# Attention scores of two heads as two 64-row tiles of TensorE, with queries that carry no zero rows

## The reference

```
q, k, v = split(einsum('bsd,od->bso', layernorm(x), w_project))
att = einsum('bhqd,bhkd->bhqk', q, k) / sqrt(16)
att = where(key > query, -1e9, att)
out = einsum('bhqk,bhkd->bhqd', softmax(att), v)
x   = x + einsum('bsd,od->bso', heads_joined(out), w_out)
```

## Time and profile before

| | |
|---|---|
| three runs, us | 1108.15, 1111.14, 1112.74 |
| median, us | 1111.14 |
| span of the profiled execution, us | 1107.3 |
| TensorE busy | 1029.0 us, 93% |
| VectorE busy | 714.0 us, 64% |
| ScalarE busy | 447.6 us, 40% |
| attention phase, us of the span | 379.6 to 845.0 |

### The profile page before, as it was taken

How to read it: one execution, slowest core, us unless ns; L and a number is a source line. 1 busy time by engine, 2 the same in 40 slices (tenths; PEclk the granted TensorE clock), 3 DMA queues, 4 the chain that set the end, 5 groups by cost and what they waited for, 6 DMA issues and landing times.

```text
span 1107.3 us, 16107 instructions
## 1 busy us (share of the span) xinstructions
PE 1029.0 (93%) x6208; PEld 473.7 (43%) x6208; DVE 714.0 (64%) x1128; ACT 447.6 (40%) x859; POOL 119.3 (11%) x147
## 2 busy tenths in 40 slices
PE   1779999999999599999999999999999999999998
PEld 1335545454555344333333333333324454544544
DVE  4786273654645588888887898887802836546362
ACT  1324020211214256555567666677786212112020
POOL 3665410000133000100000000000000100001000
PEclk9988999999999799999999999999999999999999
DMA  7000000000019600200020000000000000000000
GB/s 234 0 1 1 1 1 1 0 0 1 1 38 141 136 11 2 30 2 1 1 31 2 1 1 2 1 2 1 1 1 1 1 1 20 1 19 0 20 1 20
DMA packets 21964, 20.19 MB, mean 18 GB/s; under 512 B 4232, under 2 KB 21640, under 8 KB 21896
## 3 DMA queue, kind: packets, MB, share of 16 engines
q1 hardware_dynamic: 19784, 17.17, 7.5%
q10 hardware_dynamic: 2112, 2.10, 0.6%
HBM read 12.78 MB, written 6.29 MB: 17 GB/s over the span
## 4 chain that ended last, share of the span: by engine, by line
PE 82%; DVE 9%; issue 2%; POOL 2%; DMA 2%; ACT 1%; SPq 0%; DVEq 0%; ACTq 0%; POOLq 0%
PE ps L1037 12%; PE ps L940 10%; PE ps L1001 10%; PE ps L1023 10%; PE ps L908 10%; PE ps L909 10%; PE ps L910 10%; PE ps L941 5%; DVE m_part L820 4%; PE ps L1010 2%; DMA qk_split<-wreg 2%; PE ps L902 1%; PE ps L893 1%; PE ps L969 1%; DVE oT L626 1%
## 5 line engine op out<-in xcount | busy, mean ns | idle before, releaser
L563 ACT ACTIVATE wreg<-ps 128x512 f32<-128x512 f32 (+3 forms) x640 | 304.1, 536 | 152.9 <-PE ps L1023 78.0
L820 DVE TENSOR_REDUCE m_part<-ps 128x1 f32<-128x1024 f32 (+7 forms) x320 | 326.6, 1060 | 58.2 <-PE ps L1010 29.9
L519 ACT ACTIVATE wreg<-ps,gelu_in 128x512 f32<-128x512 f32 x128 | 88.0, 687 | 351.5 <-PE ps L910 351.5
L1023 PE MATMUL ps<-qreg,kreg 128*128 128x512 f16 (+3 forms) x640 | 181.0, 351 | 10.4 <-DMA qreg<-m_rows 8.7
L691 DVE SCALAR_TENSOR_TENSOR wreg<-ps,kappa,wreg 128x512 f32<-128x512 f32 x128 | 96.0, 750 | 145.6 <-PE ps L910 145.5
L1001 PE MATMUL ps<-kreg,qreg 128*128 128x512 f16 (+3 forms) x640 | 175.3, 351 | 7.7 <-DVE m_part L820 5.6
L940 PE MATMUL ps<-wd,qreg 128*128 128x512 f16 x512 | 166.8, 379 | 0.0
L1037 PE MATMUL ps<-wreg,v 128*17 128x512 f32 (+3 forms) x1280 | 149.8, 534 | 0.8 <-ACT oT L493 0.8
L941 PE MATMUL ps<-wd,qreg 128*128 128x256 f16 x512 | 139.6, 273 | 0.0
L1023 PEld LDWEIGHTS ps<-qreg,kreg 128*128 128x128 f16 x640 | 58.9, 97 | 131.1 <-ACT wreg L563 91.4
L908 PE MATMUL ps<-xT,wg 128*128 128x512 f16 x256 | 98.8, 386 | 3.1 <-DVE xT L671 2.4
(11 more groups left out here) (126 smaller groups left out, 931.4 us busy)
## 6 DMA issues: line engine op xcount, KB each, us to landing
qk_split<-wreg SPq DMA_DIRECT2D x4, 1024.0 KB, 9.1
kreg<-qk_split SPq DMA_DIRECT2D x24, 128.0 KB, 4.1
qreg<-qk_split SPq DMA_DIRECT2D x24, 128.0 KB, 7.8
xres<-in_L_attn_x ACTq DMA_DIRECT2D x4, 512.0 KB, 7.6
out_x<-xres SPq DMA_DIRECT2D x4, 512.0 KB, 2.9
kreg<-in_L_ffn_gate_W_packed SPq DMA_DIRECT2D x1, 1024.0 KB, 6.8
kreg<-in_L_ffn_up_W_packed SPq DMA_DIRECT2D x1, 1024.0 KB, 9.3
kreg<-in_L_ffn_down_W_packed SPq DMA_DIRECT2D x1, 1024.0 KB, 10.2
```

The costliest lines, as they stand in the source:

```text
L519: act.activation(gelu_ring[:, n % 3, :], bank(n % 2), ACT.Gelu_apprx_tanh, scale=gelu_in[:, 0:1]).then_inc(s_gelu, 1)
L563: act.activation(wreg[:, b % 8, 0:CT - q0], bank(score_bank[b], CT - q0), ACT.Exp, scale=EXP_SCALE).then_inc(s_p, 1)
L820: dve.tensor_reduce(m_part[:, r, part, col:col + 8 * (cnt - 1) + 1:8], src, AX.X, ALU.max)\
L1023: last = pe.matmul(dst, kreg[:, pair, P * j:P * j + P], qreg[:, c % 2, h % 2, pair, q0:CT], start=True, stop=not diag)
```

## The change

A matmul of scores no longer contracts all 128 partitions. It takes the 48 rows (50 with the maximum) of its own head, on partitions 0 to 63 or 64 to 127, and two such matmuls, one a head of the pair, stand next to each other in the program with their results in two banks. The mask is added in the same way, in two halves of 64 rows for each head: four matmuls of 64 columns a pair, in place of two of 128. Queries are stored once, in the first half of `inter`; the zeroing of line 465 and the transfers of line 322 go, and the first query load waits for the last products of feed-forward 1 instead. On GpSimd the small constants take ten `affine_select` in place of three. A unit of maxima is now always the two heads of a pair over at most 512 keys (`w` columns each), and the maxima of `c + 1` parts are joined by one reduction in "negate". In a step the two pairs of heads are the parts, with `weighted_values` between them. On the diagonal, both exponentials of a pair are released together, behind the masks.

```diff
-            units = []
-            for q in range(TPC):
...
+            return [(TPC * c + q, hp, CT * part, min(CT, P * (TPC * c + q + 1) - CT * part), part)
+                    for q in range(TPC) for part in range(c + 1) for hp in range(2)]
...
-                    sp.wait_ge(s_qzero, 1)
+                    sp.wait_ge(s_down_done, 1 + TPC * NCH)
...
-                if job == NCH + 1:
-                    pool.wait_ge(s_down_done, 1 + TPC * NCH)
-                    pool.memset(qflat.bitcast(i32), 0).then_inc(s_qzero, 1)
-                    pool.wait_ge(s_qzero, 1)
...
-                    if c >= 2:
-                        own(dve.tensor_tensor(m, m, m_part[:, r, 1, :], ALU.max))
+                    if c:
+                        m = m_all[:, r, :]
+                        own(dve.tensor_reduce(m, m_part[:, r, 0:c + 1, :].rearrange("p j k -> p k j"), AX.X, ALU.max))
...
+                    for a in range(2):
+                        rows = slice(64 * a, 64 * a + 3 * HD)
+                        last = pe.matmul(bank(at + a, w), qreg[rows, c % 2, pair, q0:q0 + P], kreg[rows, pair, k0:k0 + w],
+                                         start=True, stop=part < c)
+                    if part == c:
+                        last = masked([bank(at + a, P, diag) for a in range(2)], tri_a)
...
-                return pe.matmul(dst, tri[:, :], big_id[:, :], start=False, stop=True)
-
-            def scores(t, h):
+                for u in range(2):
+                    for a in range(2):
+                        rows = slice(64 * a, 64 * a + 64)
+                        last = pe.matmul(dst[a][:, 64 * u:64 * u + 64], tri[rows, u, :], big_id[rows, :],
+                                         start=False, stop=u == 1)
+                return last
+
+            def scores(t, hp):
...
+                for a in range(2):
+                    b = GH * t + 2 * hp + a
+                    if last_in_bank[b] is not None:
+                        pe.wait_ge(s_p, last_in_bank[b] + 1)
...
+                    rows = slice(64 * a, 64 * a + 3 * HD + 2)
+                    dst.append(bank(score_bank[b], CT - q0))
+                    last = pe.matmul(dst[a], kreg[rows, pair, P * j:P * j + P], qreg[rows, c % 2, pair, q0:CT],
+                                     start=True, stop=j < TPC * c)
+                    if j < TPC * c:
+                        last.then_inc(s_score, 1)
+                if j >= TPC * c:
+                    masked(dst, tri_b).then_inc(s_score, 2)
...
-                parts = [lambda: (scores(t, 0), scores(t, 1)), lambda: scores(t, 2), lambda: scores(t, 3)]
+                parts = [lambda: scores(t, 0), lambda: scores(t, 1)]
                 if t:
-                    parts.insert(2, lambda: weighted_values(t - 1))
+                    parts.insert(1, lambda: weighted_values(t - 1))
```

More of the change, by code:

```diff
@@ L151, in macaron_block @@
         s_qstack = [sem(f"query_stacks_in{k}") for k in range(NCH)]
-        s_qzero = sem("query_stacks_zeroed")
         s_slot, s_slot_read = sem("slot_written"), sem("slot_read")
@@ L191, in max_units @@
         def max_units(c, g):
-            units = []
-            for q in range(TPC):
[L197 to L211, removed]
+            return [(TPC * c + q, hp, CT * part, min(CT, P * (TPC * c + q + 1) - CT * part), part)
+                    for q in range(TPC) for part in range(c + 1) for hp in range(2)]
         def columns(unit):
-            return sum(k1 - k0 for _, _, k0, k1 in unit[2][0]) + 128
+            return 2 * unit[2][3] + 128
         def step_columns(t):
@@ L317, in load_queries @@
                         r = 64 * half + HD * row
-                        sp.dma_start(qreg[r:r + HD, c % 2, half, :, :],
+                        sp.dma_start(qreg[r:r + HD, c % 2, :, :],
                                      stack_source(c, 0, half, (0, 1, 0)[row])).then_inc(s_qstack[c], 16)
-                    if c >= 2:
[L321 to L324, removed]
             sp.wait_ge(s_ones, 1)
@@ L813, in maxima @@
                 else:
[L814 to L821, removed]
+                    i, hp, _, width, part = unit
+                    src = ps[:, 512 * at:512 * at + 1024].rearrange("p (a n) -> p a n", a=2)[:, :, 0:width]
+                    col = TPC * hp + i % TPC
+                    dve.tensor_reduce(m_part[:, r, part, col:col + 9:8], src, AX.X, ALU.max).then_inc(s_slot_read, 1)
                     read[0] = slot[0] + 1
@@ L990, in planned @@
                 else:
-                    if g == 0 and unit[2][1:3] == (0, 0) and unit[2][0] == 0:
+                    i, hp, k0, w, part = unit
+                    if g == 0 and unit[0:3] == (TPC * c, 0, 0):
                         pe.wait_ge(s_kstack[c], 16 * 6)
-                        pe.wait_ge(s_qstack[c], 16 * (6 if c < 2 else 8))
-                    for k, (h, i, k0, k1) in enumerate(unit[0]):
-                        pair = 2 * g + h // 2
-                        for m in range(k0, k1, 512):
-                            w = min(512, k1 - m)
-                            dst = bank(at + k + (m - k0) // 512, w)
-                            diag = P * i - m
-                            q0 = P * (i - TPC * c)
-                            last = pe.matmul(dst, qreg[:, c % 2, h % 2, pair, q0:q0 + P], kreg[:, pair, m:m + w],
-                                             start=True, stop=not 0 <= diag < w)
-                            if 0 <= diag < w:
-                                last = masked(dst[:, diag:diag + P], tri_a)
+                        pe.wait_ge(s_qstack[c], 16 * 6)
+                    pair = 2 * g + hp
+                    q0, diag = P * (i - TPC * c), P * i - k0
+                    for a in range(2):
[4 more added lines that the diff above has]
+                        last = masked([bank(at + a, P, diag) for a in range(2)], tri_a)
                 last.then_inc(s_slot, 1)
```

55 lines of the change are left out of this document (23 added, 32 removed).

## The result

The change made the kernel slower by 0.6%: 1115.6 us against 1110.4 us, medians of 11 runs each, ratio 1.0059 with a 95% interval of 1.0043 to 1.0075. The medians lie 5.2 us apart; 0.59% would be 6.5. I had forecast 1108 us and no change. The 11 runs go with the granted clock of TensorE over the span: the fastest, 1112.3 us, has 0.972, and the slowest, 1124.2 us, 0.957.

The account below looks back on a forecast made before the run. Bound by TensorE in regular groups, VectorE nearly as full in some stretches, ScalarE in the last group. Terms -3.4 - 3 - 4 + 7 + 0 = -3.4 us on 1111.1 gave about 1108 us, range 1102 to 1115 (8 in 10: 1086 to 1130).

Parts of the forecast that it names:

- Overlap of the pairs: Attention's score and unit matmuls on TensorE: two 64-row matmuls run together, a pair costing 0.216 us instead of 0.43.
- The rival that denied it: Attention's matmul pairs: no overlap, narrow matmuls cost by number; 1149 us, or 1125 with half of it; chance 0.22.
- The chain of waits: Full attention steps: weighted values wait for head 3's exponential, 2.78 us against 2.81 before, so the saved 0.87 becomes waiting.
- VectorE was not the bound: Rival in attention: a shorter chain lets TensorE's slack reach the maxima, VectorE bounds; 1070 us, likelier 1090; chance 0.34.
- my signs for it: Full steps: last head of weighted values waits about 0.6 us, TensorE's attention share 75% or less, step 2.75 to 2.9 us.
- The last group: Attention's last group, where ScalarE is full: ScalarE idles 0.52 us a full step; +7 us, bounds 0 and +11.
- full steps -3.4: 84 full steps outside the last group, in chunks 1 to 3: -0.04 us each, -3.4 in all, bounds -12 and +21.
- diagonal ones 11 x -0.2: Diagonal steps, four a group: -0.2 us in each of 15 groups, -3 in all, bounds -9 and +8.
- Stretches that VectorE fills: Three groups with `o`, `split`, `project`: -1 us each; denser steps of chunks 0 to 2: -1; sum -4, bounds -15 and 0.
- the clock as a rival: Attention on TensorE: granted clock falls for a third of the phase as its busy share drops; +65, 1175 us; chance 0.04.
- Before attention: Stretch before attention: zeroing of 6.93 us goes, but the transfer queue sets the end; 0 us, bounds -1.5 and 0.

Follow-up runs that it names:

- e2: The kernel before, with full-height matmuls and zero padding, given only the new order of scores and weighted values: 1133.5 us, ratio to before 1.0226.
- e3: The changed kernel, with weighted values behind both pairs of scores in the last group alone: 1108.1 us, ratio to before 0.9996.
- e10: The changed kernel, with every score matmul of chunk 0 issued twice to give TensorE more work: 1116.2 us, ratio to before 1.0063.
- e8: The changed kernel, with the old zeroing back on GpSimd and the old wait of the first query load: 1118.9 us, ratio to before 1.0083.
- e1: The changed kernel with the old order in a step, all on 64-row tiles: 1084.2 us, ratio to before 0.9769.

## Why the prediction was wrong, point by point

- *Overlap of the pairs*: right, 0.22 us a pair of 512 columns. The rival that denied it is out.
- *The chain of waits*: right, and it is the reason why the saving vanished. Forecast 2.78 us a full step, 2.82 with masks; measured 2.75, and 43.3 us for the regular group of chunk 3 (before 43.8). VectorE was not the bound; it idles 0.39 us a step. e2 shows the chain alone, 2.97 us in full height, where I expected 3.0. Two of my signs for it were wrong all the same. Of the 0.6 us of waiting that I put on the last head of the weighted values, they hold 0.16, and 0.40 stands at score 1's bank. And TensorE's busy share of attention is 86% (406.2 of 473.3 us), not 75% or less: in the last group it reads 36.3 of 37.0 us busy while the weighted values take twice their own time, so this share hides the waiting.
- *The last group*: right, +6.5 for +7; ScalarE's gap 0.46 us for 0.52; e3 took it away.
- *The middle*: near the forecast where the clock stayed. Of my terms about -9 fell on it (full steps -3.4, diagonal ones 11 x -0.2, VectorE's stretches about -3.5), and it gave -5.0 in the profiled run, but -4.5 in e3, -6.5 in e10 and -8.1 in e8, which have the same program there. The difference lies in groups with short spells of the lower clock: the first group of chunk 2 took 39.5 us at 0.96 and 38.3 at 1.00 (e8, e10), its third 34.8 at 0.95 and 33.6 at 1.00, and the first of chunk 1 29.1 at 0.93 and 28.0 at 1.00. With the shortest time of each group the middle would be at -8.6. So what is missing here belongs to the next point.
- *Chunk 0, and TensorE's clock*: this is the step that failed. In "Stretches that VectorE fills" I gave chunk 0 a part of -1, and the diagonal term another -0.8; it took +6.4 in the profiled run and +4.0 and +5.1 in e3 and e8, which are the same program up to there. What I had left out is that TensorE, finishing sooner in a stretch bound by VectorE, ran at a lower granted clock there (0.60 in group 2, where the kernel before has 1.00), and weighted values that take 1.84 us in place of 0.98 then starve VectorE (1.69 us idle). How much of group 2's loss is the clock and how much the order stays open. I had the clock as a rival, but with gaps of half a microsecond I didn't expect it; I priced it for a third of the phase, +65 us, and gave it 4%. It came in short stretches and cost a few microseconds.
- *Before attention*: normalisation came 1.5 us sooner and the queue set the start, as worked out, but my bounds of -1.5 and 0 missed. The profiled run has +2.1, of which 1.1 is feed-forward 1 ending later, which varies by more than that between the traces. Counted from the normalisation ahead of the zeroing, attention starts after 57.5 us (56.5 before), and after 56.6 to 58.0 in all ten tiled kernels without the zeroing. In that stretch the third chunk's store of 1 MB, which the key loads wait for, took 12.6 us in place of 10.5 (before, then changed):

```profile
355.80 0.43 SPq L330 DMA_DIRECT2D qk_split<-wreg  x1
366.31 2.67 SPq L308 DMA_DIRECT2D kreg<-qk_split  x6
```
```profile
355.98 0.79 SPq L308 DMA_DIRECT2D qk_split<-wreg  x1
368.62 2.67 SPq L291 DMA_DIRECT2D kreg<-qk_split  x6
```

  This is no accident of one run. The store took 10.4 and 10.5 us in the two full-height kernels (before, e2) and 12.0 to 12.7 in all eleven tiled ones, e8 with its zeroing among them. So it comes with the change, though not from the missing zeroing, and the cause is open.
- *A slip*: for half of the rival without overlap I wrote 1125 us; half of its 38 us on 1111 is 1130. It changes no chance.

With chunk 0 at +4 to +5 the sum comes near what was measured: +4.5 - 5.0 + 6.5 = +6.0 without the start, against 5.2 by the medians and 6.5 by the ratio. Against my sum of -3.4, chunk 0 (-1.8 forecast) is the largest part of the miss.

The bias behind it: I took the order of the change as given and never priced the tiles with the old order. e1 would have been a rival worth stating: the loop through three banks, 2.70 by the sum that I wrote before e1, was shorter than the one that I was adding up.

## What to carry to other kernels

When matmuls get cheaper, add up the loop of waits through banks and readers before counting the work saved: here the same tiles were 2.3% faster or 0.6% slower by where the weighted values stood. Put the consumer of an engine's last result behind enough other work to cover that engine's latency, and keep pieces that wait for a slot out of the loop. And look where the freed engine will wait for another one in short stretches: TensorE's granted clock went down in such a stretch here.

## What the runs showed of the hardware

- Two 64-row tiles on partitions 0 to 63 and 64 to 127, with results in two banks, run fully side by side: pairs of 512 columns follow each other at 0.22 us. Four mask matmuls of 64 columns take 0.06 us a pair of heads (783.97 to 784.03 below), half of what two of 128 took.

```profile
783.97 0.22 PE L983 MATMUL ps<-big_id,tri_a 64*128 64x64 f16 x4
784.03 0.38 PE L999 MATMUL ps<-inter,kreg 50*128 50x512 f16 x2
```

- TensorE's clock fell in chunk 0 after waits of 0.66 and 0.84 us, with TensorE busy 8.4 of the 11.3 us before. The Trainium skill (TensorE: Matmul & The Clock Gate, "Why this matters for your kernels") names idle gaps of more than about 3 us; the rows show a fall without any such gap, and here the measurement decides. In the second group of chunk 1 it stayed at 1.00 with TensorE busy 18.7 of 23.9 us, so these rows don't say what it asks for. The group before the fall, and that one:

```profile
397.00:408.30 11.30, 8.41 (x121) 3.40 (x115) 8.73 (x13) 6.56 (x18) 0.00 (x0) 0.99 0.11 24
467.20:491.10 23.90, 18.70 (x202) 7.08 (x201) 20.52 (x30) 14.87 (x34) 3.63 (x7) 1.00 0.01 2
```
